# Latent attention of a six-phase perceiver kernel: two products per score block in place of three

## The chip, the core and the metric

The kernel runs on one core of a Trainium2 chip. The metric is the device time of one launch in microseconds (us); lower is better. The time given is the median over runs of the same kernel. A core has a matrix engine (TensorE, in the profile PE, with its weight loads as PEld), a vector engine (VectorE, DVE), a scalar engine (ScalarE, ACT), a general one (GpSimd, POOL) and queues that start transfers (here SyncE's, SP).

## The reference

The input x has 16 sequences of 32 rows of 256 numbers, 512 rows in all. Six layers follow each other, each added to x: cross-attention, differential attention, a feed-forward layer, again cross-attention, latent attention, and a feed-forward layer. Only the fifth is changed. It reads:

```
q_c   = rmsnorm(x @ wq_down) * q_norm_w                 # 512 x 192
kv_c  = rmsnorm(x @ wkv_down) * kv_norm_w               # 512 x 64, the latent
q     = q_c @ wq_up   (16 heads x 128) ;  q_rope = rope(q_c @ wq_rope)   (16 heads x 64)
k, v  = kv_c @ wkv_up (16 heads x (128 + 128)) ;  k_rope = rope(x @ wk_rope)   (one head of 64)
s     = (q k' + q_rope k_rope') / sqrt(192), causal within each sequence
out   = softmax(s) v, heads side by side, @ wo
```

## The kernel before

**Layout.** The program has six phases, x0, a0, f0, x1, m1, f1, one for each layer. Each engine has its own instruction stream, written by hand, and semaphores tie them together; what stands first in an engine's stream runs first. There is no scheduler behind it. All of m1 is the function `mla`.

**Folding.** The 64-wide latent serves as key and value of every head. So for each head the kernel multiplies wq_up and the key part of wkv_up into one 192 x 64 matrix (and the value part with wo into a 64 x 256 matrix), before it has any activations. `fold` (PE) does it for a pair of heads, `copy_fold` (ACT) moves the result out of PSUM. Eight pairs make 16 heads; folds 0 and 1 lie inside the last item of x1, folds 2 to 6 near its end, fold 7 in m1.

**Latents.** `down` projects the rows, `latent_rows` and `rope_rows` (DVE) scale them and rotate the key, `turn_latents` (PE) turns the 128-row tiles so that features lie on partitions, first three tiles (HEAD), then the last (LAST), and `copy_latents` (ACT) and `turned_latents` (DVE) move them to SBUF. Keys exist three times: the latent, the rotated key, and the rotated key with its halves exchanged in the way that the sine needs. Each is 64 wide and stands twice, on partitions 0 to 63 and 64 to 127, once for each head of a pair.

**Queries.** `queries(pe, j, i)` makes, for pair j and all 512 rows, two banks: one with the rope queries of both heads (64 partitions each, L1723 and L1728) and one with the latent queries of both (L1726 and L1729). ACT copies the latent bank to `ql` (L1838), DVE multiplies the rope bank by cosine and by sine into `qcos` and `qsin` (L1868, in `rotate`).

**Scores.** A sequence has 32 rows, so a score block is 32 x 32. For each tile t of 128 rows (four sequences) and each head c of the pair, `scores` (L1747) adds three products for each sequence: ql, qcos and qsin, each 64 rows deep, 32 columns, 32 moving columns. That is 24 products a tile and pair. f32 products take two passes, so the trace shows 48. Between the tiles of pair j stand the query products of pair j+2, or, in the last two pairs, output products (`out_rows`, L1766). Ahead of a pair's blocks stand two products that write the causal mask (L1737).

**Around the scores.** `softmax` (DVE) of pair j: maximum (L1877), subtract (L1879), then the rotation for pair j+2, then after ACT's exponential the sum, reciprocal, product (L1882 to L1886), and four transposes (L1891). PE's order is scores(j), values(j-1) (L1758), out_rows(j-2), scores(j+1). scores(j+1) waits for the subtraction of pair j.

## Time and profile before

| | us |
|---|---|
| median of 3 runs | 731.47 |
| lowest, highest | 729.82, 732.44 |
| the profiled execution, as timed | 730.61 |
| its span (first to last instruction) | 728.8 |
| PE busy | 683.2 (94%) |
| DVE busy | 419.5 (58%) |
| ACT busy | 279.1 (38%) |
| POOL busy | 76.5 (10%) |
| mean granted TensorE clock | 0.994 of 2.4 GHz |

The profiled execution lies 0.86 us under the median. In it the stretch of m1 from the first turned tile (613.1 us) to the start of f1's norm (695.4 us) takes 82 us, 11% of the span. Busy time counts an engine as busy from the start of an instruction to its modelled end; several passes on PE overlap, so the time that a group of them costs is read from start to start.

### The profile page before, as it was taken

What the parts mean: (1) busy time and instruction counts of PE and PEld (TensorE: products, weight loads), DVE (VectorE), ACT (ScalarE), POOL (GpSimd) and SP (SyncE); (2) the same over time, 40 slices, a digit from 0 to 9 for tenths busy, and PEclk for the clock granted to TensorE, in tenths of its full rate; (3) what the DMA queues carried; (4) which work ended last, traced back from release to release, by engine and by line L of the source; (5) the groups of instructions that cost most, each with busy time, mean ns of one, the idle gap of its engine ahead of it and who ended that gap; (6) DMA issues with size and microseconds to landing.
All of it is one profiled execution on the core that took longest, in us unless ns stands there. A gap on an engine that the chain in (4) does not pass through costs nothing.

```text
span 728.8 us, 21897 instructions
## 1 busy us (share of the span) xinstructions
PE 683.2 (94%) x9706; PEld 450.7 (62%) x9706; DVE 419.5 (58%) x976; ACT 279.1 (38%) x508; POOL 76.5 (10%) x139
## 2 busy tenths in 40 slices
PE   5999999999997899999988979999999998899876
PEld 3656566656665667777766546676676775356654
DVE  5224447566565555555553692554977775355567
ACT  1334434434343233333422844444344454111125
POOL 1020000001000111111111332000201002000000
PEclk9999999999999999999999999999999999999999
DMA  6232101012300810000001510111291000000000
GB/s 191 87 149 36 58 31 31 31 60 85 121 2 2 289 31 31 30 31 30 2 1 59 204 58 30 61 32 59 79 301 58 2 4 1 3 4 4 3 1 30
DMA packets 39358, 42.26 MB, mean 58 GB/s; under 512 B 12704, under 2 KB 29856, under 8 KB 39008
## 3 DMA queue, kind: packets, MB, share of 16 engines
q1 hardware_dynamic: 39264, 40.86, 17.9%
q8 instruction: 77, 1.26, 0.7%
q14 instruction: 17, 0.14, 0.1%
HBM read 40.33 MB, written 0.52 MB: 56 GB/s over the span
## 4 chain that ended last, share of the span: by engine, by line
PE 80%; DVE 13%; ACT 3%; issue 2%; DMA 1%; POOL 1%; SPq 0%; DVEq 0%; POOLq 0%; ACTq 0%
PE psum L363 14%; PE psum L369 13%; PE psum L1048 7%; PE psum L430 5%; PE psum L383 4%; PE psum L408 4%; PE psum L397 4%; PE psum L1095 4%; PE psum L1054 4%; PE psum L1747 2%; PE psum L1079 2%; PE psum L1766 2%; DVE arena L1372 1%; PE psum L1068 1%; PE psum L1726 1%
## 5 line engine op out<-in xcount | busy, mean ns | idle before, releaser
L363 PE MATMUL psum<-arena 128*128 128x512 f32 x256 | 125.8, 618 | 10.4 <-DMA ident<-in_ident 8.1
L369 PE MATMUL psum<-arena 128*128 128x256 f32 x512 | 123.4, 386 | 0.0
L369 PEld LDWEIGHTS psum<-arena 128*128 128x128 f32 x512 | 93.2, 190 | 20.8 <-issue 8.2
L363 PEld LDWEIGHTS psum<-arena 128*128 128x128 f32 x256 | 45.6, 194 | 55.0 <-issue 41.8
L628 ACT ACTIVATE arena<-arena 128x512 f32<-128x512 f32 x64 | 48.6, 806 | 71.1 <-DVE arena L750 71.1
L430 PEld LDWEIGHTS psum<-arena 128*17 128x17 f32 x4096 | 39.3, 96 | 35.5 <-issue 30.3
L622 ACT ACTIVATE arena<-psum,arena 128x512 f32<-128x512 f32 x64 | 42.5, 687 | 37.9 <-DVE arena L737 37.8
L737 DVE TENSOR_REDUCE arena<-psum 128x1 f32<-128x512 f32 x64 | 42.4, 684 | 22.7 <-PE psum L383 22.6
L750 DVE TENSOR_SCALAR arena<-psum 128x512 f32<-128x512 f32 x64 | 41.2, 685 | 22.4 <-PE psum L397 20.2
L1048 PE MATMUL psum<-y_cols,arena 128*128 128x512 f32 x112 | 52.2, 599 | 0.0
L430 PE MATMUL psum<-arena 128*17 128x32 f32 x4096 | 48.6, 195 | 1.8 <-DVE arena L773 0.5
L1143 ACT ACTIVATE arena<-psum 128x512 f32<-128x512 f32 x48 | 28.6, 597 | 50.4 <-PE psum L1048 31.7
L309 POOL TENSOR_TENSOR arena<-arena,head_mask 128x128 f32<-128x128 f32 x64 | 24.8, 411 | 216.4 <-PE psum L383 123.4
L602 ACT ACTIVATE arena<-psum,arena 128x512 f32<-128x512 f32 x41 | 28.0, 683 | 33.5 <-PE psum L363 33.4
L397 PE MATMUL psum<-arena 64*128 64x128 f32 x512 | 37.2, 285 | 1.4 <-POOL arena L309 1.4
L604 ACT ACTIVATE arena<-psum 128x512 f32<-128x512 f32 x41 | 24.3, 593 | 36.0 <-PE psum L369 36.0
L742 DVE COPY arena<-psum 128x512 f32<-128x512 f32 x32 | 22.1, 689 | 27.5 <-PE psum L408 27.0
L397 PEld LDWEIGHTS psum<-arena 64*128 64x128 f32 x512 | 31.1, 187 | 10.8 <-issue 7.0
L408 PEld LDWEIGHTS psum<-ident,arena 128*128 128x128 f32 x256 | 28.7, 141 | 14.1 <-issue 12.3
L383 PE MATMUL psum<-arena 64*128 64x512 f32 x128 | 36.1, 641 | 0.0
L408 PE MATMUL psum<-ident,arena 128*128 128x128 f32 x256 | 34.1, 276 | 0.8 <-ACT arena L622 0.8
L634 ACT ACTIVATE arena<-psum 128x512 f32<-128x512 f32 x32 | 19.1, 596 | 39.3 <-PE psum L408 38.9
(232 smaller groups left out, 997.9 us busy)
## 6 DMA issues: line engine op xcount, KB each, us to landing
arena<-in_ctxT SPq DMA_DIRECT2D x32, 512.0 KB, 3.7
arena<-in_L_attn_Wv SPq DMA_DIRECT2D x1, 2048.0 KB, 8.3
arena<-in_L_attn_Wq SPq DMA_DIRECT2D x8, 256.0 KB, 2.9
arena<-in_L_attn_Wk SPq DMA_DIRECT2D x8, 256.0 KB, 3.4
arena<-in_L_attn_Wo SPq DMA_DIRECT2D x1, 2048.0 KB, 11.5
arena<-in_L_ffn_w_gating SPq DMA_DIRECT2D x1, 2048.0 KB, 7.6
arena<-in_L_attn_wo SPq DMA_DIRECT2D x1, 2048.0 KB, 11.0
arena<-in_wq_upT SPq DMA_DIRECT2D x1, 1536.0 KB, 8.6
```

Of the source, the lines that this page charges most:

```text
L363: last = nc.tensor.matmul(bank, wkv[:, c, i * P:(i + 1) * P], x[:, c, :], start=(c == 0), stop=(c == NC - 1))
L369: last = nc.tensor.matmul(bank[:, kk * D:(kk + 1) * D], x[:, c, k * P:(k + 1) * P], wkv[:, c, D:2 * D], start=(c == 0), stop=(c == NC - 1))
L383: nc.tensor.matmul(S[r], qbd[b % 2][a, h, :, :].rearrange("p j q -> p (j q)"), kT[home(b)][a, h, :], start=True, stop=True).then_inc(s_sco ...
L397: ins = nc.tensor.matmul(S[2 * kp + r][:, (2 * kk + h) * P:(2 * kk + h + 1) * P], kT[home(b)][a, h, k * P:(k + 1) * P], qbd[b % 2][a, h, : ...
L408: last = nc.tensor.transpose(T[g % 2][:, k * P:(k + 1) * P], pr[g % 2][:, k * P:(k + 1) * P], e.ident)
L430: last = nc.tensor.matmul(O[b % 2][j * SQ:j * SQ + VW, g * SQ:(g + 1) * SQ], va[home(b)][:, k, HG * g + j, :], probs[:, j * SQ:(j + 1) * S ...
L622: nc.scalar.activation(pr[g % 2], S[g % 2], ACT.Exp, bias=nmx[:, g:g + 1]).then_inc(s_exp, 1)
L628: nc.scalar.activation(pTk[b % 2][k], clip[k // 2][:, k % 2, :], ACT.Exp, bias=mb[:, b, k:k + 1], scale=m01[:, b, k:k + 1]).then_inc(s_exp, 1)
L737: nc.vector.tensor_reduce(nmx[:, g:g + 1], S[g % 2], AX.X, ALU.max, negate=True).then_inc(s_mx, 1)
L750: nc.vector.tensor_scalar(dst, S[i].rearrange("p (a n) -> p a n", n=P), 50.0, -50.0, ALU.min, ALU.max)\
L1048: last = nc.tensor.matmul(bank, w[:, c, f], e.yT[:, c, :], start=(c == 0), stop=(c == NC - 1))
L1054: last = nc.tensor.matmul(bank[:, (t % 2) * 2 * DV:(t % 2 + 1) * 2 * DV], e.yT[:, c, t * P:(t + 1) * P], wv[:, c, p * 2 * DV:(p + 1) * 2 * ...
```

## The change

Each head of a pair now has its own query bank of 128 partitions: 64 latent queries and under them 64 rope queries. On the key side the latent and the rotated key stand above each other in `kT[:, 0]`; `kT[:, 1]` keeps the exchanged key. A score block adds one product of 128 rows (latent and cosine together) and one of 64 rows (sine, on partitions 64 to 127), 16 products a tile and pair.

To get there, the query weights are laid out by head (`wq0`, `wq1`; the rope weights arrive with a stride, in 256-byte pieces), the fold's second product writes both halves of the bank's partitions, one transposed tile, one key copy on ACT and one row copy and one rotated sum on DVE are dropped, and ACT's `copy_query` is gone: DVE multiplies all 128 partitions by a table that holds ones for the latent half and cosines for the other, and the lower 64 partitions by the sine, for each head. The rotation of the second head of pair j+2 stands at the end of `softmax(j)`. Three banks serve the queries in turn. One more small load and one more split load are issued by SP.

```diff
-    wr = early([P, 2, H * ROPE])
+    wq0, wq1 = early([P, PAIRS, 4, KR]), early([P, PAIRS, 2, KR])
...
-    wl = late([P, PAIRS, 2, P])
...
-    qcT, kT = late([P, 2, ROWS]), late([P, 3, ROWS])
+    qcT, kT = late([P, 2, ROWS]), late([P, 2, ROWS])
...
+    place = lambda i: heads[:, i * ROWS:(i + 1) * ROWS]
+    both, turned = ([[place(4 * u + 2 * k + i) for i in range(2)] for u in range(3)] for k in range(2))
...
-    FOLD, DOWN, QRB, QLB, OB, ACC = (B[0], B[1]), (B[2], B[3], B[4], B[5]), (B[5], B[1]), B[0], B[2], (B[6], B[7])
+    FOLD, DOWN, QB, OB, ACC = (B[0], B[1]), (B[2], B[3], B[4], B[5]), (B[0], B[1], B[5]), B[2], (B[6], B[7])
...
-                         (wr[:, 0, :], d.wq_rope_halves[0:P, :]), (wr[0:QR1, 1, :], d.wq_rope_halves[P:QR, :])):
+                         (wq0[:, :, 1::2, :], d.wq_rope_halves[0:P, :].rearrange("p (j i w) -> p j i w", i=2, w=ROPE)),
+                         (wq1[half(0), :, 1, :], rope_of(0)), (wq1[half(1), :, 1, :], rope_of(1))):
...
-            nc.tensor.matmul(bank[half(1), P + KR * i:P + KR * (i + 1)], wqu[:, h, P:QR], wuk[:, h, :], start=True, stop=True)
+            nc.tensor.matmul(bank[half(i), P:P + KR], wqu[:, h, P:QR], wuk[:, h, :], start=True, stop=True)
...
-            for i in range(3):
-                ins = nc.tensor.transpose(LAT[k][2 + i][:, r], krow[:, i, t, :], e.ident)
+            for i in range(2):
+                ins = nc.tensor.transpose(LAT[k][2 + i][:, r], krow[:, t, i * KR:i * KR + P], e.ident)
...
 
-        cols = slice(j * P, (j + 1) * P)
-        if i == 0:
-            wait(pe, s_rope, 2 * (j - 1))
-            nc.tensor.matmul(QRB[j % 2], wr[:, 0, cols], qcT[:, 0, :], start=True, stop=False)
-        elif i == 1:
-            wait(pe, s_q_act, j)
-            nc.tensor.matmul(QLB, wl[:, j, 0, :], qcT[:, 0, :], start=True, stop=False)
+        n = 2 * j + i
+        if i < 2:
+            wait(pe, s_rope, 2 * (n - 2))
+            nc.tensor.matmul(QB[n % 3], wq0[:, j, 2 * i:2 * i + 2, :].rearrange("p a w -> p (a w)"), qcT[:, 0, :],
+                             start=True, stop=False)
         else:
-            nc.tensor.matmul(QRB[j % 2], wr[half(0), 1, cols], qcT[half(0), 1, :], start=False, stop=True).then_inc(s_qr, 1)
-            nc.tensor.matmul(QLB, wl[half(1), j, 1, :], qcT[half(1), 1, :], start=False, stop=True).then_inc(s_ql, 1)
+            for i in range(2):
+                nc.tensor.matmul(QB[(2 * j + i) % 3], wq1[half(i), j, :, :].rearrange("p a w -> p (a w)"), qcT[half(i), 1, :],
+                                 start=False, stop=True).then_inc(s_q, 1)
 
     def scores(pe, j):
 
-        pe.wait_ge(s_q_act, j + 1)
-        pe.wait_ge(s_rope, 2 * j + 2)
+        u = j % 3
+        pe.wait_ge(s_rope, 4 * j + 4)
         wait(pe, s_sub, j)
...
-            for i, q in enumerate((ql, qcos, qsin)):
+            for i, rows in enumerate((slice(0, P), half(1))):
                 for c in range(2):
                     for k in range(BPT):
                         r = slice(t * P + k * SQ, t * P + (k + 1) * SQ)
-                        last = nc.tensor.matmul(B[3 + c][k * SQ:(k + 1) * SQ, t * SQ:(t + 1) * SQ], q[j % 3][half(c), r],
-                                                kT[half(c), i, r], start=False, stop=(i == 2 and t == NT - 1))
+                        last = nc.tensor.matmul(B[3 + c][k * SQ:(k + 1) * SQ, t * SQ:(t + 1) * SQ],
+                                                (both, turned)[i][u][c][rows, r], kT[rows, i, r],
+                                                start=False, stop=(i == 1 and t == NT - 1))
         last.then_inc(s_scores, 1)
...
-        nc.scalar.activation(wl[:, j, 0, :], bank[:, 0:P], ACT.Copy).then_inc(s_wf, 1)
-        nc.scalar.activation(wl[half(1), j, 1, :], bank[half(1), P:2 * P], ACT.Copy).then_inc(s_wf, 1)
+        nc.scalar.activation(wq0[:, j, 0::2, :], bank[:, 0:P].rearrange("p (i w) -> p i w", i=2), ACT.Copy).then_inc(s_wf, 1)
+        nc.scalar.activation(wq1[:, j, 0, :], bank[:, P:P + KR], ACT.Copy).then_inc(s_wf, 1)
...
-        nc.scalar.activation(kT[:, 0, cols], LAT[k][2], ACT.Identity, scale=vvec).then_inc(s_kv_act, 1)
-        nc.scalar.activation(kT[:, 1, cols], LAT[k][3], ACT.Copy).then_inc(s_kv_act, 1)
-
-    def copy_query(act, j):
-        if j >= PAIRS:
-            return
-        act.wait_ge(s_ql, j + 1)
-        wait(act, s_scores, j - 2)
-        nc.scalar.activation(ql[j % 3], QLB, ACT.Copy).then_inc(s_q_act, 1)
+        nc.scalar.activation(kT[:, 0, cols], LAT[k][2], ACT.Identity, scale=vhalf).then_inc(s_kv_act, 1)
...
-    def rotate(v, j):
+    def rotate(v, j, i):
 
         if j >= PAIRS:
             return
-        v.wait_ge(s_qr, j + 1)
+        n = 2 * j + i
+        v.wait_ge(s_q, n + 1)
         wait(v, s_scores, j - 2)
         blocks = lambda x: x.rearrange("p (n q) -> p n q", q=SQ)
-        for i, dst in enumerate((qcos, qsin)):
-            nc.vector.tensor_tensor(blocks(dst[j % 3]), blocks(QRB[j % 2]), rope[:, i, :].unsqueeze(1).to_broadcast([P, NB, SQ]),
-                                    ALU.mult).then_inc(s_rope, 1)
+        for k, rows in enumerate((slice(0, P), half(1))):
+            w = rows.stop - rows.start
+            nc.vector.tensor_tensor(blocks((both, turned)[k][j % 3][i][rows]), blocks(QB[n % 3][rows]),
+                                    rope[rows, k, :].unsqueeze(1).to_broadcast([w, NB, SQ]), ALU.mult).then_inc(s_rope, 1)
 
...
-        rotate(v, j + 2)
+        rotate(v, j + 2, 0)
...
             nc.vector.transpose(pT[u][a:a + 32].rearrange("p c t k -> p (c t) k")[:, :, a:a + 32],
                                 flat(pr[a:a + 32])).then_inc(s_pT, 1)
+        rotate(v, j + 2, 1)
...
-        twice = lambda x: x.unsqueeze(2).to_broadcast([P, n, 2, ROPE])
-        for i in range(2):
-            a = slice(i * ROPE, (i + 1) * ROPE)
-            e.ch.mark(nc.vector.tensor_tensor(krow[:, 1 + i, at, :].rearrange("p t (u f) -> p t u f", u=2),
-                                              twice(t1[:, at, a]), twice(t2[:, at, a]), ALU.add))
+        e.ch.mark(nc.vector.tensor_tensor(krow[:, at, KR:], t1[:, at, :], t2[:, at, :], ALU.add))
...
-        for i in range(2):
-            e.ch.mark(nc.vector.tensor_tensor(krow[:, 0, at, i * KR:(i + 1) * KR], e.psum[:, 2 + ts[0]:3 + ts[-1], QR:QR + KR],
-                                              rr[:, at, 1].unsqueeze(2).to_broadcast([P, n, KR]), ALU.mult))
+        e.ch.mark(nc.vector.tensor_tensor(krow[:, at, 0:KR], e.psum[:, 2 + ts[0]:3 + ts[-1], QR:QR + KR],
+                                          rr[:, at, 1].unsqueeze(2).to_broadcast([P, n, KR]), ALU.mult))
...
-        rotate(v, 0)
-        rotate(v, 1)
+        for n in range(4):
+            rotate(v, n // 2, n % 2)
...
-    a["rope_cols"] = np.stack([np.tile(cos.T, (4, 1)), np.tile(sin.T, (4, 1))], 1)
+    a["rope_cols"] = np.stack([np.concatenate([np.ones((2 * HR, SQ), np.float32), np.tile(cos.T, (2, 1))]), np.tile(sin.T, (4, 1))], 1)
```

The instruction order on PE, pair 0, first two tiles, before (L1737 mask, L1747 scores, L1723 and L1726 query products of pair 2):

```order
L1737 MATMUL psum<-arena 128x128 x2
L1747 MATMUL psum<-arena 32x32 x24
L1723 MATMUL psum<-arena 128x512
L1747 MATMUL psum<-arena 32x32 x24
L1726 MATMUL psum<-arena 128x512
```

and after (L1739 mask, L1749 scores, L1726 and L1730 query products):

```order
L1739 MATMUL psum<-arena 128x128 x2
L1749 MATMUL psum<-arena 32x32 x16
L1726 MATMUL psum<-arena 128x512
L1749 MATMUL psum<-arena 32x32 x16
L1726 MATMUL psum<-arena 128x512
```

Each run of 24 score products has become one of 16, of which the first eight are 128 rows deep and the last eight 64; the query products between them keep their places and number.

On DVE, the softmax of pair 1 before (L1868 is the rotation):

```order
L1877 TENSOR_REDUCE arena<-psum 128x8
L1879 TENSOR_TENSOR arena<-psum,arena 128x256
L1868 TENSOR_TENSOR arena<-psum,arena 128x512 x2
L1882 TENSOR_REDUCE arena<-arena 128x8
L1884 RECIPROCAL arena<-arena 128x8
L1886 TENSOR_TENSOR arena<-arena 128x256
L1891 STREAM_TRANSPOSE arena<-arena 32x8x32 x4
```

and after (L1862 is the rotation):

```order
L1871 TENSOR_REDUCE arena<-psum 128x8
L1873 TENSOR_TENSOR arena<-psum,arena 128x256
L1862 TENSOR_TENSOR arena<-psum,arena 128x512
L1862 TENSOR_TENSOR arena<-psum,arena 64x512
L1876 TENSOR_REDUCE arena<-arena 128x8
L1878 RECIPROCAL arena<-arena 128x8
L1880 TENSOR_TENSOR arena<-arena 128x256
L1885 STREAM_TRANSPOSE arena<-arena 32x8x32 x4
L1862 TENSOR_TENSOR arena<-psum,arena 128x512
L1862 TENSOR_TENSOR arena<-psum,arena 64x512
```

Two rotation products of 512 elements have become four, two of them at the end of the pair, behind the transposes.

## Rows read from the trace of the kernel before

**Rows 1.** The page: of part 4 the engines, of part 5 the group of L430.
```profile
PE 80%; DVE 13%; ACT 3%; issue 2%; DMA 1%; POOL 1%; SPq 0%; DVEq 0%; POOLq 0%; ACTq 0%
...
L430 PE MATMUL psum<-arena 128*17 128x32 f32 x4096 | 48.6, 195 | 1.8 <-DVE arena L773 0.5
```

**Rows 2.** Timeline, pair 1: start, duration, engine, line, operation, shapes, count, idle before.
```profile
641.78 0.62 PE L1747 MATMUL psum<-arena 64*32 64x32 f32 x48
642.34 1.13 PE L1723 MATMUL psum<-arena 128*128 128x512 f32 x2
643.39 0.62 PE L1747 MATMUL psum<-arena 64*32 64x32 f32 x48
```

**Rows 3.** Timeline, pair 6: two score blocks in a row.
```profile
677.39 1.02 PE L1747 MATMUL psum<-arena 64*32 64x32 f32 x96
678.35 1.13 PE L1766 MATMUL psum<-arena 128*128 128x256 f32 x4
```

**Rows 4.** Timeline, cross-attention: products of 128 rows by 17 columns, then another shape.
```profile
591.35 0.73 PE L430 MATMUL psum<-arena 128*17 128x32 f32 x64
592.01 0.66 PE L1677 MATMUL psum<-arena 128*128 128x64 f32 x4
```

**Rows 5.** A stretch of L430 alone: length, busy us (passes that run in it).
```profile
591.34:591.47 0.13, 0.12 (x16) 1.00 0.00 0
```

**Rows 6.** Timeline, first cross-attention: sixteen passes, then 128 rows again, or 64.
```profile
14.47 3.62 PE L369 MATMUL psum<-arena 128*128 128x256 f32 x16
17.92 3.60 PE L363 MATMUL psum<-arena 128*128 128x512 f32 x8
...
41.45 3.61 PE L369 MATMUL psum<-arena 128*128 128x256 f32 x16
44.99 1.13 PE L383 MATMUL psum<-arena 64*128 64x512 f32 x4
```

**Rows 7.** Timeline, one fold late in the second cross-attention.
```profile
605.04 0.27 PE L1680 MATMUL psum<-arena 128*64 128x64 f32 x1
...
605.32 0.60 PE L1683 MATMUL psum<-arena 128*64 128x256 f32 x3
```

**Rows 8.** Timeline, from the last norm of the cross-attention to the first query.
```profile
608.98 0.40 DVE L142 TENSOR_SCALAR y_rows<-x_rows,ln_mean_var,ln_rstd 128x256 f32<-128x256 f32 x1
610.04 0.44 PE L158 MATMUL psum<-ident,y_rows 128*128 128x128 f32 x2
...
615.61 0.55 PE L1715 MATMUL psum<-ident,arena 128*128 128x128 f32 x3
...
617.14 0.49 ACT L1831 ACTIVATE arena<-psum 128x384 f32<-128x384 f32 x1
...
618.55 0.33 PE L1711 MATMUL psum<-ident,arena 128*128 128x128 f32 x1 [1.19 <-ACT arena L1807]
...
620.28 0.28 ACT L1831 ACTIVATE arena<-psum 128x128 f32<-128x128 f32 x1
...
620.70 1.39 PE L1723 MATMUL psum<-arena 128*128 128x512 f32 x2 [0.97 <-ACT arena L1831]
```

**Rows 9.** Timeline, pair 1 on DVE: maximum, rotation, transposes; and the next maximum.
```profile
640.59 0.43 DVE L1877 TENSOR_REDUCE arena<-psum 128x8 f32<-128x256 f32 x1 [1.72 <-PE psum L1747]
...
641.39 1.28 DVE L1868 TENSOR_TENSOR arena<-psum,arena 128x512 f32<-128x512 f32 x2
...
643.79 1.84 DVE L1891 STREAM_TRANSPOSE arena<-arena 32x256 f32<-32x256 f32 x4
...
647.28 0.42 DVE L1877 TENSOR_REDUCE arena<-psum 128x8 f32<-128x256 f32 x1 [1.65 <-PE psum L1747]
```

**Rows 10.** Stretch: length, busy us (count) of PE, PEld, DVE, ACT, POOL; clock; DMA.
```profile
621.40:624.80 3.40, 3.40 (x7) 0.84 (x5) 0.00 (x0) 0.00 (x0) 0.00 (x0) 0.50 0.00 0
```

**Rows 11.** Timeline, SyncE's transfers for the latent attention.
```profile
526.78 7.64 SPq L1649 DMA_DIRECT2D arena<-in_wkv_upT  x2
...
536.98 2.65 SPq L1649 DMA_DIRECT2D arena<-in_wq_rope_halves  x2
```

More of the change, by code:

```diff
@@ L1594, in mla @@
                                  "qcT_act", "qcT_dve", "kvT_act", "kvT_dve", "zero", "mask"))
-    (s_prep, s_wf, s_qr, s_ql, s_q_act, s_rope, s_scores, s_sub, s_exp, s_soft, s_pr, s_pT, s_pv, s_oT, s_rows) = (
-        sem(f"m1_{n}") for n in ("fold", "fold_act", "q_rope", "q_lat", "q_act", "rope", "scores", "sub", "exp", "softmax",
+    (s_prep, s_wf, s_q, s_rope, s_scores, s_sub, s_exp, s_soft, s_pr, s_pT, s_pv, s_oT, s_rows) = (
+        sem(f"m1_{n}") for n in ("fold", "fold_act", "queries", "rope", "scores", "sub", "exp", "softmax",
                                  "probs", "pT", "pv", "oT", "out_rows"))
@@ L1606, in mla @@
     mask32, identm = early([P, 2, P]), early([P, 2, P], BF16)
-    wl = late([P, PAIRS, 2, P])
     wvo = late([P, PAIRS, D])
-    qc, krow = late([P, NT, QR]), late([P, 3, NT, 2 * KR])
+    qc, krow = late([P, NT, QR]), late([P, NT, KR + 2 * ROPE])
     junk = late([P, 2 * NT, QR], BF16)
@@ L1612, in mla @@
     t1, t2 = late([P, NT, 2 * ROPE]), late([P, NT, 2 * ROPE])
-    qcT, kT = late([P, 2, ROWS]), late([P, 3, ROWS])
+    qcT, kT = late([P, 2, ROWS]), late([P, 2, ROWS])
     part = lambda a, n, w: heads[:, a:a + H * w].rearrange("p (h n) -> p h n", n=w)
     wqu, wuk, wuv, wo = (part(a * H, H, w) for a, w in ((0, QR), (QR, KR), (QR + KR, KR), (QR + 2 * KR, D)))
-    ql, qcos, qsin = ([heads[:, (3 * u + i) * ROWS:(3 * u + i + 1) * ROWS] for u in range(3)] for i in range(3))
-    oT = [heads[:, (9 + u) * ROWS:(10 + u) * ROWS] for u in range(2)]
+    place = lambda i: heads[:, i * ROWS:(i + 1) * ROWS]
+    both, turned = ([[place(4 * u + 2 * k + i) for i in range(2)] for u in range(3)] for k in range(2))
+    oT = [place(12 + u) for u in range(2)]
     sc, ex = ([late([P, 2, NT, SQ]) for _ in range(2)] for _ in range(2))
@@ L1621, in mla @@
     B = e.B
-    FOLD, DOWN, QRB, QLB, OB, ACC = (B[0], B[1]), (B[2], B[3], B[4], B[5]), (B[5], B[1]), B[0], B[2], (B[6], B[7])
+    FOLD, DOWN, QB, OB, ACC = (B[0], B[1]), (B[2], B[3], B[4], B[5]), (B[0], B[1], B[5]), B[2], (B[6], B[7])
     HEAD, LAST = (0, 1, 2), (NT - 1,)
     head, last = slice(0, LAST[0] * P), slice(LAST[0] * P, ROWS)
-    LAT = ([B[i][:, head] for i in (7, 6, 2, 3, 4)],
-           [B[i][:, a * P:(a + 1) * P] for i, a in ((5, 0), (0, 0), (5, 1), (5, 2), (0, 1))])
+    LAT = ([B[i][:, head] for i in (7, 6, 2, 3)],
+           [B[i][:, a * P:(a + 1) * P] for i, a in ((5, 0), (0, 0), (5, 1), (0, 1))])
     SC = e.psum[:, 3:5, 0:NT * SQ].rearrange("p c (t k) -> p c t k", t=NT)
-    N_W, N_HEADS = 12, 6
+    N_W, N_HEADS = 13, 7
     SCALE = (NOPE + ROPE) ** -0.5
@@ L1633, in load @@
         cols = lambda a: a.rearrange("(c p) n -> p c n", p=P)
+        rope_of = lambda i: d.wq_rope_halves[P:QR, :].rearrange("p (j i w) -> p i j w", i=2, w=ROPE)[:, i]
         loads = [(wd[:, :, 0:QR], cols(d.L1_attn_wq_down)), (wd[:, :, QR:QR + KR], cols(d.L1_attn_wkv_down)),
@@ L1638, in load @@
                  (vvec[half(0), :], d.L1_attn_kv_norm_w.unsqueeze(1)), (vvec[half(1), :], d.L1_attn_kv_norm_w.unsqueeze(1)),
+                 (vhalf[half(0), :], d.L1_attn_kv_norm_w.unsqueeze(1)),
                  (cosr, d.rope_rows[0]), (sinr, d.rope_rows[1]), (rope, d.rope_cols),
@@ L1757, in values @@
             for c in range(2):
-                last = nc.tensor.matmul(OB[half(c), t * P:(t + 1) * P], krow[:, 0, t, 0:KR], pT[u][:, c, t, :],
+                last = nc.tensor.matmul(OB[half(c), t * P:(t + 1) * P], krow[:, t, 0:KR], pT[u][:, c, t, :],
                                         start=True, stop=True)
@@ L1783, in pe @@
         pe.wait_ge(s_kv_dve, 2)
-        pe.wait_ge(s_kv_act, 4)
+        pe.wait_ge(s_kv_act, 2)
         for j in range(2):
@@ L1849, in act @@
         copy_latents(act, 1)
-        copy_query(act, 0)
-        copy_query(act, 1)
         for j in range(PAIRS):
@@ L1929, in during_x1_dve @@
             v.wait_ge(s_w, 16 * N_W)
+            nc.vector.memset(vhalf[half(1), :], 1.0)
             nc.vector.tensor_copy(identm, mask32).then_inc(s_mask, 1)
@@ L1940, in turned_latents @@
         nc.vector.tensor_scalar(qcT[:, 1, cols], LAT[k][1], qnw[:, 1:2], None, ALU.mult).then_inc(s_qc_dve, 1)
-        nc.vector.tensor_copy(kT[:, 2, cols], LAT[k][4]).then_inc(s_kv_dve, 1)
+        nc.vector.tensor_copy(kT[:, 1, cols], LAT[k][3]).then_inc(s_kv_dve, 1)
     def dve(v, done):
```

3 lines of the change are left out of this document (1 added, 2 removed).

## The prediction

> **What bounds the kernel now.** I read the chain of waits first: 80% of the span hangs on PE and 13% on DVE [rows 1]. So a change pays where PE has fewer or shorter instructions, or where PE waits for something that gets shorter. The next view is the timeline of the changed phase. In the pairs PE runs without a gap: a score block starts at 641.78, the query product behind it at 642.34, the next block at 643.39 [rows 2]. A block of 48 passes therefore costs 0.56 us and a query product 1.05. The start of a group counts, not the 0.62 busy time, since passes overlap. Ahead of the pairs PE waits twice for ACT, 1.19 us for the fold's copies and 0.97 for the keys' copies [rows 8]. DVE works on pair 1 from 640.59 to 645.63 and starts on the next at 647.28, when PE has its scores [rows 9]: it has 1.65 us to spare a pair.
>
> **Score blocks.** A block loses 8 of 24 products, but the 16 left are no longer of one shape: 8 are 128 rows deep, 8 are 64 deep, both 32 columns wide. First what a block is made of. Two blocks in a row take 0.96 [rows 3], one takes 0.56, so 48 further passes cost 0.40, 8.3 ns each, and about 0.16 is the change of shape around the block. Then the new shape. The trace has no product of 128 rows by 32 columns. The nearest is L430, 128 rows by 17 columns with 32 moving, on the same four column places: its first 16 passes lie in 0.12 us [rows 5], all 64 in 0.66 [rows 4]. The last of them starts at 591.35 + 0.73 - 0.19 (a single pass [rows 1]) = 591.89, and the next shape at 592.01: leaving costs 0.12. So a group of 16 passes costs 0.12 + 0.12 = 0.24.
>
> The second half of the block is such a group again, if going from 128 to 64 rows counts as a change of shape. Sixteen L369 passes take 3.45 us when the same depth follows and 3.54 when 64 rows follow at the same column width [rows 6]: 0.09 more, so it does. The Trainium skill says the same ("TensorEngine Tiling (Array Packing)", Tiling Modes: a change of the tiling mode, not of the tile, drains the engine); without that drain the block would come to 0.36. The trace agrees with the rule.
>
> A block then costs 2 x 0.24 = 0.48 against 0.56, and 0.08 is saved. There are 28 single blocks (four in each of pairs 0 to 5, two in pairs 6 and 7): 28 x 0.08 = 2.2 us. The doubled block in pairs 6 and 7 becomes four groups, 0.96, what it costs now: nothing. Bounds: with a free change inside the block it takes 32 x 8.3 ns + 0.16 = 0.43, and the doubled one 0.69, together 28 x 0.13 + 2 x 0.27 = 4.2 saved. At the other end weights are not loaded behind the stream. 32 columns stream in 27 ns (a 256-column pass takes 3.45/16 = 0.216 [rows 6]); load and stream one after the other on four places instead of eight are 54/4 = 13.5 ns a pass, a group 0.34, a block 0.68, a doubled one 1.36: 28 x 0.12 + 2 x 0.40 = 4.2 lost. I take the 2.2, since L430 is the row nearest in shape. Against the upper end stands also L1680: four passes with 64 columns loaded and 64 moving, all on the same place, take 0.28 with another pass between them [rows 7], where unhidden loads would need 4 x 0.108 = 0.43.
>
> **Folds.** The second product of a fold puts its two heads on both column halves, not on one. Its four passes now take 0.28 in a row, 70 ns each; two by two they save between 0.11 and 0.14. I take 0.11. Five folds (2 to 6) stand in a row on PE ahead of the norm's turn L158, whose rows are ready at 608.98 + 0.40 = 609.38 while it starts at 610.04 [rows 8]. So all of 5 x 0.11 = 0.55 us comes through, and the 0.66 between the two is the cap. Folds 0 and 1 lie before a wait for ACT and give nothing. Bounds 0 and 0.66.
>
> **Latents.** One turned tile of three goes: (0.55 - 0.27)/2 = 0.14 at most, I take 0.12, three times up to the tiles' end. ACT's third key copy goes too (from 617.14 on, about 0.4). The two together would be 0.7, but then fold 7 on PE is what ACT waits for, and I leave 0.55 for the start of L1711, now 618.55 [rows 8]. Behind it one more turned tile (0.12), and the queries no longer wait for the copy that ends at 620.56 but for the one before it, 0.2 earlier. Sum 0.55 + 0.12 + 0.2 = 0.85 us; bounds 0.4 (the copies hide in fold 7) and 1.1. The row copy and the rotated sum that DVE loses stand beside PE work and give nothing else.
>
> **First queries.** The second bank of pair 1 reuses the first bank, so it waits for the rotation of pair 0's first head: two DVE products, 1.28 us [rows 9], plus 0.1 of signalling. PE has one query product of 1.05 in that time. That adds 0.35; bounds 0 and 0.8 (1.28 twice, less two query products). Later the same wait, for a rotation that begins after the subtraction, has two blocks and one query product before it, 0.48 x 2 + 1.05 = 2.0 us, and needs 1.3: hidden.
>
> **DVE.** A pair gets two more rotation products, 1.28 us: 5.04 + 1.28 = 6.32. The period of pairs 0 to 2 is 647.28 - 640.59 = 6.69 now, and 6.69 - 4 x 0.08 = 6.37 after. It fits with 0.05 us to spare; from pair 2 on PE has output products as well and the period is longer. Cost 0; without that cover 0.3 at two pairs. Half of the rotation stands behind the transposes, where PE does not wait for it before the pair after the next. The last two pairs have no rotation, so the tail behind the last scores is as it was. ACT loses the query copies; nothing waits there now.
>
> **Transfers.** The rope weights come in 256-byte pieces. The two value and key loads in such pieces hold SyncE's queue for 7.64 us, the two rope loads now 2.65 [rows 11]. I estimate 6 for the three new ones. They start at 537 and the first fold at 592.01 [rows 4]: hidden many times over.
>
> **Clock.** From 621.40 to 624.80 the granted clock is 0.50, that is 1.2 GHz, behind the two PE gaps of 1.19 and 0.97 us [rows 8, 10]; it costs up to 1.7 us. The change shortens both gaps, which may spare it in some runs, or may not: I count 0, and 1.7 as the lower end.
>
> **Sum.** -2.2 - 0.55 - 0.85 + 0.35 = -3.25 us on the profiled execution's 730.61: 727.4. That execution lies 0.86 under the median of the three runs, so the forecast for the median is 728.2.
>
> **The rivals.**
> A. The blocks give nothing: the change of shape and dearer passes eat the eight products. 16 passes then take 0.16 in place of 0.12. For it speaks that L430 loads 17 columns and not 32, against it that its passes keep to the stream's 27 ns by four. Only folds, latents and queries remain: -1.05, 730.4.
> B. Slower: half the places. A 64-row product of 32 columns has eight places in the array, one of 128 rows or all on the lower 64 rows has four. If load and stream on a place do not overlap there, a block costs 0.68: +4.2 - 1.05 = +3.15, 734.6. It outweighs the other terms from 11 ns a pass on. Against it L430 and L1680 as above. The Trainium skill's rule on tiling ("TensorEngine Tiling (Array Packing)", Tiling Modes) speaks for this side: with 8 tiles for 24 products and 4 for 16, a block streams for 4 product times in place of 3. But the 8.3 ns a pass of rows 2 and 3 are well above 27/8 = 3.4, so streaming does not bound the old block.
> C. The slow stretch of the clock goes as well: -3.25 - 1.7, 726.5.
> D. DVE becomes the bound of pairs 0 to 2: -3.25 + 0.3 to 0.6, about 728.7.
>
> **How the numbers follow.** Forecast 0.48, A 0.25, B 0.09, C 0.13, D 0.05. A measurement of this kernel can tell 0.3%, 2.2 us, from no change: under 729.3 is faster, over 733.7 slower. Forecast (0.45 of its 0.48), C and D are faster, 0.63; A and the rest 0.28; slower is B, 0.09. The range goes from below C (725.9) to above A with the runs' spread (731.9).
>
> **What would show it.** In the changed profile a single score block followed by a query product takes 0.48 from start to start, and the passes of its first half 0.12; 0.56 or more is A, 0.65 or more B. A fold takes 0.11 less, L158 starts 0.55 earlier, the first query about 1.4 earlier. PE waits some 0.35 before the second query product of pair 1. In pairs 1 and 2 DVE has almost no idle time before the maximum; if PE waits there for the subtraction longer than now, it is D. The forecast is wrong as a whole if the time goes up while the blocks are shorter: then a wait that I have at nothing has come in.

## The result and the profile after

| | before | after |
|---|---|---|
| median, us | 729.8 (6 runs) | 726.12 (6 runs) |
| lowest, highest | 728.18, 732.44 | 725.61, 726.89 |
| profiled execution, its span | 730.61, 728.8 | 726.38, 724.6 |
| DVE busy | 419.5 | 430.8 |
| ACT busy | 279.1 | 271.9 |

The ratio is 0.9943 with a 95% interval of 0.9927 to 0.9958: 0.6% faster. The forecast was 728.2, with a range of 725.9 to 731.9. The time is inside, 2.1 us under the forecast. Part of that is the base. The kernel before gave 731.47 over the three runs shown first, 729.8 over six and 729.27 over 23 later ones. The change in time is about -3.7 by the medians and -4.2 by the two profiled executions, where -3.25 was forecast. That looks close, and it hides four terms that were wrong and offset each other.

The page of the profile after, engines and chain (of before [rows 1]):

```profile
PE 679.8 (94%) x9189; PEld 446.8 (62%) x9190; DVE 430.8 (59%) x988; ACT 271.9 (38%) x498; POOL 76.8 (11%) x139
...
PE 80%; DVE 13%; ACT 3%; issue 2%; DMA 1%; POOL 1%; SPq 0%; DVEq 0%; ACTq 0%; POOLq 0%
```

PE has lost 3.4 us of busy time and still carries 80% of the chain, DVE 13% as before. So the kind of bound is the same, and the place to look is PE's order in time.

The timeline of the kernel after, pair 1 and the pair behind it: a score block, a query product, the next block (answers to [rows 2]).

```profile
641.24 0.59 PE L1749 MATMUL psum<-arena 128*32 128x32 f32 x32
...
641.76 1.12 PE L1726 MATMUL psum<-arena 128*128 128x512 f32 x2
...
642.82 0.59 PE L1749 MATMUL psum<-arena 128*32 128x32 f32 x32
```

A block and its query product now take 1.58 us where 1.61 stood. The block alone is 641.76 - 641.24 = 0.52, against 0.56 before and 0.48 forecast. Pair 7 has the doubled block (answers to [rows 3]):

```profile
680.26 1.11 PE L1749 MATMUL psum<-arena 128*32 128x32 f32 x64
...
681.30 1.13 PE L1769 MATMUL psum<-arena 128*128 128x256 f32 x4
```

It takes 1.04, against 0.96 before. What the block consists of shows in three stretches of the kernel after, counted for the score passes alone. The columns are the stretch (from:to), its length, busy us of PE and of PEld with the passes that run in it, clock, DMA share and GB/s.

```profile
641.24:641.38 0.14, 0.14 (x16) 0.14 (x16) 1.00 0.00 0
641.24:641.50 0.26, 0.26 (x16) 0.22 (x16) 1.00 0.00 0
641.50:641.64 0.14, 0.14 (x25) 0.14 (x16) 1.00 0.00 0
```

The 16 passes of the first shape have all started within 0.14 us. Until 641.50 no other starts: that is the change from 128 rows to 64, 0.12 us. From there 16 new ones start within 0.14, while nine old ones still count as running. To the query product at 641.76 it is 0.12 again. So the block is 0.26 + 0.26.

Folds, two starts in a row in the kernel after, and then the way to the first query (answers to [rows 7, 8]):

```profile
605.16 0.66 PE L1680 MATMUL psum<-arena 128*128 128x64 f32 x4
...
606.45 0.66 PE L1680 MATMUL psum<-arena 128*128 128x64 f32 x4
```

```profile
609.03 0.44 PE L158 MATMUL psum<-ident,y_rows 128*128 128x128 f32 x2
...
610.23 1.74 PE L1694 MATMUL psum<-arena,y_cols 128*128 128x448 f32 x4 [0.77 <-ACT y_cols L166]
...
616.38 0.33 PE L1714 MATMUL psum<-ident,arena 128*128 128x128 f32 x1 [0.77 <-ACT arena L1810]
...
618.28 1.96 PE L1726 MATMUL psum<-arena 128*128 128x512 f32 x4 [0.84 <-ACT arena L1833]
```

A fold takes 1.29. L158 starts at 609.03 instead of 610.04. The last tile's first product L1714 waits 0.77 for ACT instead of 1.19, and the first query 0.84 instead of 0.97.

Where the 4.2 us of the two traces are, by starts on PE (the row of pairs 6 and 7 ends at the value products behind the last block):

| stretch | before | after | change | forecast |
|---|---|---|---|---|
| start to fold 2 | 603.16 | 602.69 | -0.47 | 0 |
| fold 2 to L158 | 6.88 | 6.34 | -0.54 | -0.55 |
| L158 to the first query product | 10.66 | 9.25 | -1.41 | -0.85 |
| first query product to pair 0's mask | 7.47 | 6.54 | -0.93 | +0.35 |
| pairs 0 to 5 | 47.46 | 48.14 | +0.68 | -1.92 |
| pairs 6 and 7 | 11.50 | 9.93 | -1.57 | -0.32 |
| the rest | 41.65 | 41.67 | +0.02 | 0 |

Two rows carry the clock. Before, the stretch at 1.2 GHz lay in the first queries [rows 10]. After, it lies in pair 1 (columns as in [rows 10]):

```profile
632.90:636.30 3.40, 3.40 (x43) 1.22 (x46) 3.17 (x8) 0.00 (x0) 0.00 (x0) 0.50 0.00 0
```

The same lines at full clock are in the traces of other kernels below: the unchanged first queries take 5.82 us (so 1.65 of the 7.47 is the clock), and the changed pairs 0 to 5 take 46.81 (so 1.33 of the 48.14 is). At full clock the first queries cost +0.72 and pairs 0 to 5 give -0.65. The first row of the table lies ahead of everything changed. Both traces have one other slow stretch there, so it is neither the change nor the clock. It differs by more from one execution to the next: 601.99 in a second trace of the kernel before, which has no slow stretch there, and 604.46 in that of pad128, which has one.

### The profile page after: what moved, and what is told of

Same layout as the page of the kernel before. It is cut to its first block, busy times and chain, and to the rows that moved or that the text cites. A ratio compares the mean times of both kernels' runs of the same rounds, so it can differ in the third digit from the quotient of the medians.

```text
span 724.6 us, 20867 instructions
## 1 busy us (share of the span) xinstructions
PE 679.8 (94%) x9189; PEld 446.8 (62%) x9190; DVE 430.8 (59%) x988; ACT 271.9 (38%) x498; POOL 76.8 (11%) x139
## 4 chain that ended last, share of the span: by engine, by line
PE 80%; DVE 13%; ACT 3%; issue 2%; DMA 1%; POOL 1%; SPq 0%; DVEq 0%; ACTq 0%; POOLq 0%
PE psum L363 14%; PE psum L369 14%; PE psum L1048 7%; PE psum L430 5%; PE psum L383 4%; PE psum L408 4%; PE psum L397 4%; PE psum L1095 4%; PE psum L1054 4%; PE psum L1749 2%; PE psum L1726 2%; PE psum L1079 2%; PE psum L1769 2%; DVE arena L1372 1%; PE psum L1068 1%
## 5 line engine op out<-in xcount | busy, mean ns | idle before, releaser
L369 PE MATMUL psum<-arena 128*128 128x256 f32 x512 | 125.0, 390 | 0.4 <-ACT arena L602 0.4
L430 PEld LDWEIGHTS psum<-arena 128*17 128x17 f32 x4096 | 39.3, 96 | 35.7 <-issue 30.3
L430 PE MATMUL psum<-arena 128*17 128x32 f32 x4096 | 48.6, 195 | 2.0 <-ACT arena L628 0.7
L1143 ACT ACTIVATE arena<-psum 128x512 f32<-128x512 f32 x48 | 28.2, 597 | 49.8 <-PE psum L1048 31.8
L604 ACT ACTIVATE arena<-psum 128x512 f32<-128x512 f32 x41 | 24.3, 594 | 38.2 <-PE psum L369 38.2
L742 DVE COPY arena<-psum 128x512 f32<-128x512 f32 x32 | 22.1, 690 | 27.4 <-PE psum L408 27.0
L615 DVE COPY arena<-psum 128x512 f32<-128x512 f32 x23 | 15.9, 690 | 31.5 <-PE psum L369 31.2
```

The source lines that it names most:

```text
L369: last = nc.tensor.matmul(bank[:, kk * D:(kk + 1) * D], x[:, c, k * P:(k + 1) * P], wkv[:, c, D:2 * D], start=(c == 0), stop=(c == NC - 1))
L430: last = nc.tensor.matmul(O[b % 2][j * SQ:j * SQ + VW, g * SQ:(g + 1) * SQ], va[home(b)][:, k, HG * g + j, :], probs[:, j * SQ:(j + 1) * S ...
```

## The experiments

Two sets of kernels were run, each beside the kernel before: its median was 729.27 over 23 runs in the first and 729.51 over 13 in the second.

**before_again.** No edit, one more execution.

> The kernel before once more, unchanged, for a second trace. The first trace of before has two stops of PE in pairs 6 and 7 that nothing in the profile explains (0.55 us inside the value products, 0.76 us inside a score block); the trace of the changed kernel has none, and there pairs 6 and 7 together are 1.6 us shorter than the blocks explain. Theory: the stops belong to this program (its instruction stream) and come again at the same two places, pair 6 from mask to mask again 6.1 us and pair 7 5.4 us. Rival: they are chance, like the stretches at half clock, and are gone or elsewhere in this trace: pair 6 then 5.6 us and pair 7 4.5 us. The half-clock stretches I expect at other places than 242.5 and 621.4 us.

729.09, span 727.3. The first queries again take 7.47, pairs 0 to 5 47.50 and pairs 6 and 7 11.09. Of the two stops that were expected again, one came. The longer one, in pair 7, is there at the same place (0.89 us; pair 7 takes 5.48, as the theory said). The shorter one, inside the value products of pair 6, is gone: they stand in one piece, a little longer than the 1.09 that they take elsewhere, and pair 6 takes 5.60, the rival's number. In the trace of copy128 it is there with 0.30. So the stop in pair 7 comes with this kernel, and the size of the one in pair 6 is a matter of the execution.

The half-speed stretch is there again too, at 620.2, where another place had been expected. It does not belong to the kernel for that: copy128 and thin_last_pairs, in which PE has the same instructions up to pair 6, have none in the latent attention.

**pad128.** The sine products also read 128 rows, the upper 64 of them zeros, so that a block has one shape.

```diff
-            for i, rows in enumerate((slice(0, P), half(1))):       # in scores
+            for i, rows in enumerate((slice(0, P), slice(0, P))):
...
-        for k, rows in enumerate((slice(0, P), half(1))):           # in rotate
+        for k, rows in enumerate((slice(0, P), slice(0, P))):
...
-    ... np.tile(sin.T, (4, 1))
+    ... np.concatenate([np.zeros((2 * HR, SQ), np.float32), np.tile(sin.T, (2, 1))])
```

> The changed kernel with the sine product 128 rows deep too: the rotation writes all 128 partitions and its table holds zeros for the latent half, so the product adds the same numbers. A block is then 32 passes of one shape. Theory 1 (the change of shape inside the block costs 0.126 us and the passes themselves are the same): a block falls from 0.52 to 0.40 us, a doubled one from 1.04 to about 0.75; 28 x 0.12 + 2 x 0.29 = 3.9 us less than the changed kernel, unless DVE becomes the bound in pairs 0 to 2 (its pair then takes 6.6 us against 6.1 of PE), which gives 0.5 to 1 us of it back: 722 to 723 us. Theory 2 (what makes the block dearer than predicted is that 16 products use four places of the array in place of eight): the passes stay slow or become slower, the block stays at 0.50 or more, no gain. On DVE: if 64 partitions cost it more than 128, the two rotations of a head take 1.28 us again in place of 1.41.

722.21 us, ratio 0.9894 (0.9871 to 0.9917). The interval lies wholly under that of the changed kernel. A block and the query product behind it in its timeline, and two stretches of that block, counted for the score passes alone:

```profile
640.40 0.46 PE L1749 MATMUL psum<-arena 128*32 128x32 f32 x32
...
640.79 1.12 PE L1726 MATMUL psum<-arena 128*128 128x512 f32 x2
```

```profile
640.40:640.66 0.26, 0.26 (x31) 0.26 (x32) 1.00 0.00 0
640.66:640.79 0.13, 0.13 (x26) 0.09 (x12) 1.00 0.00 0
```

All 32 weight loads and 31 of the 32 products have started within 0.26 us, some 8 ns each, with no gap in the middle, and leaving takes 0.13. The block takes 0.39, 0.13 less than 0.52. That is the change of shape, shown by taking it away at the same number of passes, and it is what theory 1 said (0.40, and 722 to 723 for the whole). The Trainium skill says that a change of the tiling mode drains the engine ("TensorEngine Tiling (Array Packing)", Tiling Modes); this trace agrees and puts 0.13 us on it. That half the places cost time, the other side that the prediction weighed, is true but small (next run). Pairs 0 to 5 take 43.69 in place of 46.81: 3.12, which is 24 blocks of 0.13.

**eight_places.** The sine product of head c takes rows of half c, so its four sequences and two heads lie on eight places and not on four. The first head's sine term is then formed from the wrong rows.

```diff
                 for c in range(2):
+                    rows = half(c) if i else rows
...
-        for k, rows in enumerate((slice(0, P), half(1))):           # in rotate
+        for k, rows in enumerate((slice(0, P), slice(0, P))):
```

> The changed kernel with the sine products of the first head on partitions 0 to 63 and of the second on 64 to 127, so that the second half of a block uses eight places of the array in place of four; the change of shape inside the block stays. For it the rotation writes all 128 partitions; the sine term of the first head is then formed from the wrong rows, so only the time counts. Theory 1: the block stays at 0.52 (0.50 to 0.52), as the passes come every 7 to 9 ns whatever the number of places, and the time is that of the changed kernel within 0.3 us. Theory 2: the second half runs as fast as the old blocks' first passes, the block falls to 0.48, and the time by about 1.2 us.

724.82, ratio 0.9935 (0.9917 to 0.9952), which the times can't tell from the changed kernel. The trace can:

```profile
640.25 0.55 PE L1750 MATMUL psum<-arena 128*32 128x32 f32 x32
...
640.74 1.13 PE L1726 MATMUL psum<-arena 128*128 128x512 f32 x2
```

```profile
640.25:640.50 0.25, 0.25 (x16) 0.22 (x16) 1.00 0.00 0
640.51:640.61 0.10, 0.10 (x25) 0.10 (x16) 1.00 0.00 0
```

The block takes 0.49, so theory 2 (0.48) is the nearer one. Its first half is as in the kernel after: 16 passes, and no other start until 640.50. The second half starts in 0.10 and not in 0.14. So four places cost about 0.04 more per 16 passes than eight. Pairs 0 to 5 take 45.88, 0.93 less than 46.81, or 0.039 for each of 24 blocks.

**copy128.** The kernel before, with the fold's second copy on all 128 partitions instead of on 64 (it copies rows that nobody reads).

```diff
-        nc.scalar.activation(wl[half(1), j, 1, :], bank[half(1), P:2 * P], ACT.Copy).then_inc(s_wf, 1)
+        nc.scalar.activation(wl[:, j, 1, :], bank[:, P:2 * P], ACT.Copy).then_inc(s_wf, 1)
```

> The kernel before with one edit: ACT's second copy of a fold moves all 128 partitions in place of the upper 64 (what it writes on the lower 64 is not read). In the changed kernel the three copies of a fold take 0.67 us from the start of the first to the end of the last, before 0.99, which I had not predicted. Theory: an ACT instruction on another set of partitions does not overlap its neighbours; then the three copies here take about 0.7 to 0.75 us too, the norm's copy L166 and the last latents' turn start 0.3 us earlier each, and the whole is 0.6 us faster (0.999 of before). Rival: the copies became shorter because the second has 64 elements in place of 128; then they take 0.95 or more here and the time is unchanged.

729.09, ratio 0.9993 (0.9974 to 1.0012): the time doesn't resolve it. The trace does. ACT's copies of one fold, and the norm's copy L166 behind them, first in the kernel before, then in copy128, then in the kernel after:

```profile
610.15 0.28 ACT L1805 ACTIVATE arena<-psum 128x128 f32<-128x128 f32 x1 [0.41 <-PE psum L1683]
...
610.45 0.27 ACT L1806 ACTIVATE arena<-psum 64x128 f32<-64x128 f32 x1
...
610.75 0.38 ACT L1807 ACTIVATE arena<-psum 128x256 f32<-128x256 f32 x1
611.03 0.38 ACT L166 ACTIVATE y_cols<-psum 128x256 f32<-128x256 f32 x1
```

```profile
609.46 0.28 ACT L1805 ACTIVATE arena<-psum 128x128 f32<-128x128 f32 x1 [0.68 <-PE psum L1683]
...
609.63 0.27 ACT L1806 ACTIVATE arena<-psum 128x128 f32<-128x128 f32 x1
...
609.79 0.39 ACT L1807 ACTIVATE arena<-psum 128x256 f32<-128x256 f32 x1
610.05 0.40 ACT L166 ACTIVATE y_cols<-psum 128x256 f32<-128x256 f32 x1
```

```profile
609.14 0.28 ACT L1808 ACTIVATE arena<-psum 128x128 f32<-128x128 f32 x1 [0.62 <-PE psum L1686]
609.32 0.22 ACT L1809 ACTIVATE arena<-psum 128x64 f32<-128x64 f32 x1
609.42 0.39 ACT L1810 ACTIVATE arena<-psum 128x256 f32<-128x256 f32 x1
609.68 0.40 ACT L166 ACTIVATE y_cols<-psum 128x256 f32<-128x256 f32 x1
```

The copy of 64 partitions between two of 128 starts 0.30 behind the first, and the next 0.30 behind it. With all of 128 partitions the distances are 0.17 and 0.16 for the same 128 columns. From the first copy to L166 it is 0.88, 0.59 and 0.54. Since L166 feeds the projection and fold 7's copies release the last tile's turn, both waits shrink: from fold 2 to the first query it takes 17.54 before and 17.02 in copy128. Here 0.52 us come from the number of partitions alone.

**bank4 and pad128_bank4.** The second head of pair 1 gets a bank of its own (the output's, which is free then), so its query product has no rotation to wait for. bank4 is the changed kernel with it, pad128_bank4 is pad128 with it and leaves nothing out.

```diff
+    QB4 = lambda n: B[2] if n == 3 else QB[n % 3]
...
-            wait(pe, s_rope, 2 * (n - 2))
-            nc.tensor.matmul(QB[n % 3], wq0[...
+            if n > 3:
+                wait(pe, s_rope, 2 * (n - 2))
+            nc.tensor.matmul(QB4(n), wq0[...
...
```

> The changed kernel with the fourth query bank alone, for the price of the wait that the change brought in. Theory: the stretch from the first query product to pair 0's mask falls from 6.54 (changed kernel) to 5.82 us, the price of the wait is 0.6 to 0.7 where I had predicted 0.35; time 0.6 us under the changed kernel's. Rival: it comes back in pair 0, whose query products then wait for the rotation of pair 1: pair 0 at 6.9 us or more in place of 6.5, time unchanged.

> The 128-row sine product of pad128 together with a fourth query bank: the second head's queries of pair 1 go to the bank that later takes the values' output, so they no longer wait for the rotation of pair 0's first head. Theory: from the first query product to pair 0's mask PE takes 5.8 us in place of 6.4, as in the kernel before where the clock was full, and pair 0's scores are not late, since DVE starts the same rotations at the same time: 0.5 us less than pad128, 721.7. Rival: DVE has four rotations of 1.28 us to make before pair 1 and one more head's in pair 0, so the wait only moves to the bank or the scores behind it (pair 0 gets 0.5 us longer): time as pad128.

bank4 took 725.58, ratio 0.9956 (0.9938 to 0.9974), not to be told from the changed kernel by the time. pad128_bank4 took 720.07, ratio 0.9874 (0.9851 to 0.9897): the lowest median, 6.05 us under the changed kernel's, and its interval lies wholly under that of the changed kernel. Under pad128 it is 2.14 us where 0.5 had been expected, but the intervals of these two overlap. In their profiled executions 1.37 of the 1.97 us between them lie ahead of fold 2, where nothing differs. The bank's own share is what the next rows show, 0.6. First the wait in the kernel after, then the same place in pad128_bank4 (L1729 and L1733 its query products, L1742 its mask):

```profile
621.33 2.87 DVE L1862 TENSOR_TENSOR arena<-psum,arena 128x512 f32<-128x512 f32 x4 [3.30 <-PE psum L1730]
...
622.80 1.12 PE L1726 MATMUL psum<-arena 128*128 128x512 f32 x2 [0.45 <-DVE arena L1862]
```

```profile
623.54 1.13 PE L1733 MATMUL psum<-arena 64*128 64x512 f32 x4
...
624.50 0.22 PE L1742 MATMUL psum<-arena 64*128 64x128 bf16 x2
...
624.66 0.46 PE L1752 MATMUL psum<-arena 128*32 128x32 f32 x32
```

With the wait the first queries take 6.54 (6.41 in pad128), without it 5.82, what they take in the kernel before at full clock. In bank4 they take 6.06. There the rotations of pair 0, four products in 2.86 us from 620.70, end at 623.56, and the mask starts at 623.71, 0.24 later than the products before it would let it. In pad128_bank4 four take 2.48 and end at 624.21, before the mask at 624.50. So in bank4 part of the wait seems to have moved to the mask; that is argued from the times, the profile names no releaser there. Pair 0 takes 6.66 in bank4, not the 6.9 of its rival. The wait and what it drags along cost 0.5 to 0.7 us.

**thin_last_pairs and dense_last_pairs.** The table shows 1.57 us in pairs 6 and 7 where the blocks should give nothing: four single blocks save 4 x 0.035 and two doubled ones lose 2 x 0.08. The cause had to be something else. In the kernel before PE stands still there in the middle of a run of products, and the profile shows nothing that it waits for ("issue"). The rows are L1758, the values' product, and L1747, the doubled block of pair 7, cut in two behind pass 69:

```profile
681.39 0.44 PE L1758 MATMUL psum<-arena 128*64 128x128 f32 x4 [0.55 <-issue]
...
683.68 0.79 PE L1747 MATMUL psum<-arena 64*32 64x32 f32 x69
...
685.23 0.34 PE L1747 MATMUL psum<-arena 64*32 64x32 f32 x27 [0.76 <-issue]
```

The second trace of the kernel before:

```profile
678.85 1.33 PE L1758 MATMUL psum<-arena 128*64 128x128 f32 x16
...
682.03 0.79 PE L1747 MATMUL psum<-arena 64*32 64x32 f32 x69
...
683.70 0.34 PE L1747 MATMUL psum<-arena 64*32 64x32 f32 x27 [0.89 <-issue]
```

The theory: in these pairs the short products stand so dense that PE's instructions don't arrive in time. Eight score products fewer per tile spare it. So thin_last_pairs takes the kernel before and leaves the sine product out in pairs 6 and 7, dense_last_pairs takes the changed kernel and does the sine product twice there.

```diff
-            for i, q in enumerate((ql, qcos, qsin)):                                        # thin, on the kernel before
+            for i, q in enumerate((ql, qcos, qsin) if j < PAIRS - 2 else (ql, qcos)):
...
```

```diff
-            for i, rows in enumerate((slice(0, P), half(1))):                               # dense, on the changed kernel
+            for n, i in enumerate((0, 1) if j < PAIRS - 2 else (0, 1, 1)):
+                rows = half(1) if i else slice(0, P)
...
```

> The kernel before without the sine products of pairs 6 and 7 alone (the term is left out there), so these two pairs have 16 products of one shape a block. Three traces of the old programs have PE stops of 0.8 to 1.3 us in these two pairs, and the changed kernel and its variants none. Theory: PE runs out of instructions there, because 24 products a block without long query products between them use them up faster than the 16 KB fetches bring them; with 16 a block the stops are gone, and the pairs fall by more than the 0.13 a block that 16 missing passes are worth: pair 6 5.1 us and pair 7 4.1 us from mask to mask. Rival: the stop belongs to something else in these pairs (a bank, a wait) and stays: 0.8 us or more of idle PE inside pair 7.

> The changed kernel with a third group of eight products in each block of pairs 6 and 7 (the sine products twice, so its scores there are not the reference's): as many instructions there as in the kernel before. Theory (instructions run out): a stop of 0.5 to 1 us of PE comes back in pair 6 or 7 beside the 0.07 us a block that eight more products of the same shape take. Rival: no stop, pair 7 at 4.39 + 4 x 0.07 = 4.7 us.

thin_last_pairs took 725.04 (one run), and pairs 6 and 7 take 8.74 (9.2 was expected). Its doubled block of pair 7 is whole again:

```profile
679.27 0.76 PE L1747 MATMUL psum<-arena 64*32 64x32 f32 x64
...
679.96 1.13 PE L1766 MATMUL psum<-arena 128*128 128x256 f32 x4
```

dense_last_pairs took 728.64 (one run), and pairs 6 and 7 take 12.33 against 9.93. The stop is back, in the doubled block of pair 7, behind pass 74:

```profile
679.11 0.23 PE L1739 MATMUL psum<-arena 64*128 64x128 bf16 x2 [0.33 <-DVE arena L1874]
...
680.98 1.22 PE L1750 MATMUL psum<-arena 128*32 128x32 f32 x74
...
683.13 0.39 PE L1750 MATMUL psum<-arena 64*32 64x32 f32 x22 [0.93 <-issue]
```

In dense_last_pairs the additional passes cost 4 x 0.13 (a block 0.65) and 2 x 0.26 (the doubled one 1.30), 1.04 of the 2.40; 0.07 a block had been expected. The stop has 0.93 of the rest, and most of what remains is the wait of pair 7's mask for DVE. That the stop comes and goes with the number of score products a tile is shown, once in each direction, and it is in both traces of the kernel before and in copy128's (1.04 us behind pass 69), and in none of the changed kernel, pad128, eight_places, bank4 and pad128_bank4. That the supply of instructions is what fails is an inference; no run changed the supply itself. But the traces hold more that speaks for it. The page of the kernel before has a queue that carries instructions:

```profile
q8 instruction: 77, 1.26, 0.7%
```

Those are 77 packets of 16 KB, and PE has 19412 products and weight loads, 252 for each packet. Between its two stops lie 127 products and their 127 weight loads, 254, so the stops stand about one packet apart. And by the times in the packets' records PE starts again 1.34 to 1.53 us after a packet has landed, in all six stops of the four traces: in the kernel before a packet lands at 679.86 and PE starts at 681.39, the next lands at 683.84 and PE starts at 685.23. The packets come some 4 to 6 us apart, so chance would hardly give that.

## Why the prediction was right or wrong

**The failing step is the size of the score blocks: 1.92 us forecast for the 24 blocks of pairs 0 to 5 (2.2 with the four of pairs 6 and 7), 0.65 measured.** The second is the stops of PE in pairs 6 and 7, which the prediction had at nothing without a reason, and which were worth 1.57. The two nearly cancel, and that the time came out near is luck. First the blocks. The structure held. A block is two groups, each of 16 passes and a leaving, and the change from 128 to 64 rows inside a block is real (0.12 in the kernel after, 0.13 by pad128; [rows 4, 6] gave 0.12 and 0.09). What was off is the passes: 0.14 for 16 on four places, where the prediction took over L430's: "its first 16 passes lie in 0.12 us". The count in [rows 5] was of products with 17 columns, and of passes that run in a stretch chosen to the hundredth. An error of 0.02 a group is 0.04 a block, half of the 0.08 that was to be gained. That is the trap: the gain was a small difference of two large costs, so an error of 8% in the new cost took away half of it. The doubled block was to cost nothing and costs 0.08 more, by the same error, four times 0.02.

The rest of it is rival D, at a smaller price and one place. DVE's share of a pair grew by a second rotation. In dense_last_pairs, whose pair 1 is that of the changed kernel at full clock, DVE goes from the rotation straight to the maximum, and PE waits for the subtraction at the mask behind it:

```profile
636.89 1.42 DVE L1863 TENSOR_TENSOR arena<-psum,arena 128x512 f32<-128x512 f32 x2
...
638.34 0.42 DVE L1872 TENSOR_REDUCE arena<-psum 128x8 f32<-128x256 f32 x1
...
639.37 0.23 PE L1739 MATMUL psum<-arena 64*128 64x128 bf16 x2 [0.20 <-DVE arena L1874]
```

The period of pair 1 is 6.71 there, against 6.69 in the kernel before, while pairs 2 to 5 are each 0.14 shorter than before. So in this one pair the shorter blocks give nothing, and the wait costs about 0.16 us. The forecast counted two products of a rotation as 1.28; in the changed kernel they take 1.42, and four in a row 2.87. In pad128, with 128 partitions in both, the two take 1.28 to 1.29 again, and four 2.48. So a product on 64 partitions next to ones on 128 is dearer than one on all 128.

**Folds: right.** 0.54 of 0.55, with 0.11 a fold (1.29 for 1.40 [rows 7]).

**Latents: direction right, 0.56 too small.** 0.30 of it lies between L158 and the projection, where nothing was forecast, and 0.3 more between the projection and the last tile's first product L1714. Both are ACT's: the fold's second copy now covers 128 partitions and no longer holds up its neighbours. The prediction saw in the edit of `copy_fold` only a change of layout. copy128, which has this and nothing else of the change, gives 0.52, about what was missing.

**First queries: direction right, price half.** 0.72, not 0.35. The wait for the rotation was named. But the second product starts 622.80 - 621.23 = 1.57 behind the first, where the forecast had 1.38, mostly because a head's rotation takes 1.43 here and not 1.28. And the pair stood 0.96 apart at full clock before, not 1.05. So 0.61. The other 0.11 is that behind the gap the product lasts 1.06 to the next, not 0.95. The dearer rotation is the smaller part of the miss: in pad128, where it costs what the forecast took, the wait still costs 6.41 - 5.82 = 0.59.

**Transfers at nothing: right.** In the trace of the kernel after PE waits for no load between fold 2 and the end of pair 7.

**Pairs 6 and 7: their stops were not forecast at all.** 0.32 was forecast there, from four single blocks; by their measured costs the blocks give nothing (4 x 0.035 less 2 x 0.08). The 1.57 is the stops, which stood in the trace and were not read. They are 0.55 and 0.76 of idle time; from start to start they take more: the value products with the way to the mask 1.80 against 1.17 after, the block behind the first stop 0.70 against 0.56 elsewhere, the doubled block 1.82 against 0.96. In the second trace of the kernel before the gain would have been 11.09 - 9.93 = 1.16, since the first stop was not there. [rows 3], from pair 6, lie 6 us ahead of the longer one, and the chain's "issue 2%" [rows 1] was passed over.

**Clock.** Counted as 0, and between these two traces that is nearly so: -1.65 in one place, +1.33 in another. The trace of the kernel after has the half-speed stretch 11 us later, it has not gone. So C is not what happened, though the time is near its 726.5. That the change moved it is not shown: the other seven traces have none in the latent attention, whether they keep the old order there (copy128, thin_last_pairs) or the new one. A (blocks give nothing) was the nearer description of pairs 0 to 5, which gave a third of the forecast; the block itself, 0.52, lies halfway between A's 0.56 and the forecast's 0.48. B is refuted, the block is shorter than before, and on four places 16 passes cost 0.14 where B needed 0.22. The wait of DVE that D named is real in one pair.

So the sum came out near for a wrong reason. Blocks gave 1.6 less than forecast and queries took 0.4 more; the latents gave 0.6 more, the stops 1.6, the clock 0.3, and 0.5 lies ahead of the change: -3.25 + 1.6 + 0.4 - 0.6 - 1.6 - 0.3 - 0.5 = -4.25, the -4.2 of the traces.

## What to carry to other kernels

With products as small as these, count changes of shape before products: here eight fewer products a block saved 0.04 us, and padding 64 rows with zeros to keep one shape saved 0.13. Where a gain is a small difference of two block costs, measure the new block by itself, or keep its whole error in the range. Before you price an edit, look at every idle stretch marked "issue" in the stretch that it touches, and at the partition counts of small copies on ACT and DVE.

## What was not expected of the hardware

- A change of array shape between 128 and 64 rows costs 0.12 to 0.13 us of PE, at 32 columns and 32 moving.
- 16 passes of 32 columns start in 0.14 us on four places and in 0.10 on eight; 32 of one shape on four places in 0.26.
- An ACT copy of 64 partitions between two of 128 starts 0.30 behind its neighbour and delays the next by 0.30; of 128 partitions 0.17 and 0.16. The copy itself is recorded with 0.27 in both cases.
- On DVE a rotation of one head takes 1.42 when its second product has 64 partitions, and 1.28 to 1.29 when it has 128.
- PE stood still for 0.76, 0.89, 1.04 and 0.93 us in the doubled block of pair 7, behind the same pass (69) in the three traces of kernels with the old order. Each stop ended 1.34 to 1.53 us after a 16 KB packet of instructions had landed.
- The stretch of 3.4 us at 1.2 GHz that lay at 621.4 and 620.2 in the kernel before lay at 632.9 in the kernel after. The latent attention of the other seven traces has none.
